# A mixture-of-experts layer in 48 half tiles instead of 64, with its weights loaded by SyncE

## What is computed

```python
x = hidden_states.reshape(-1, h)                      # 2048 x 512
p = jax.nn.sigmoid(x @ gate_w.T)                      # 16 experts
p = p / jnp.sum(p, axis=-1, keepdims=True)
w, idx = jax.lax.top_k(p, 2)
w = w / jnp.sum(w, axis=-1, keepdims=True)
combine = jnp.sum(one_hot(idx, 16) * w[..., None], axis=1)
gu = jnp.einsum('th,ehf->etf', x, gate_up_proj)       # 512 -> 2 x 256
gate, up = jnp.split(gu, 2, axis=-1)
inter = jax.nn.silu(gate) * up
y = jnp.einsum('eti,eih->eth', inter, down_proj)      # 256 -> 512
out = jnp.einsum('eth,te->th', y, combine)
```

## Time and profile before

| | us |
|---|---|
| median of three runs | 2494.53 |
| the profiled execution, its time | 2495.26 |
| the profiled execution, span of its records | 2495.2 |
| of it, up to the start of the expert loop | 2118 |
| the expert loop, 64 steps | 328 |
| behind the last product | 49 |

### The profile page before, as it was taken

The page is one execution under the profiler, slowest core; times in us unless marked ns, Lnnn a source line. Parts: engine busy times, 40 slices in busy tenths (PEclk is TensorE's granted clock), DMA queues, the critical chain, the costliest instruction groups (busy, mean ns, idle before and its releaser), DMA issues. The chain is left out here.

```text
span 2495.2 us, 40462 instructions
## 1 busy us (share of the span) xinstructions
PE 2258.1 (90%) x12755; PEld 1950.1 (78%) x12755; DVE 1629.1 (65%) x3963; ACT 1238.8 (50%) x3351; POOL 719.4 (29%) x1299
## 2 busy tenths in 40 slices
PE   4999999999995789977999999999999964999992
PEld 4999899999884567766888888888888852878781
DVE  5777777777778952234666666666666676666664
ACT  3545545545543112215666666666666631666661
POOL 1000100100000642223333333433333302666672
PEclk8999999999997999998999999999999986999996
DMA  6111121211101310001111111111211012566405
GB/s 232 60 66 53 59 71 63 71 59 48 65 35 31 94 32 0 0 24 61 43 51 48 70 50 42 67 42 50 72 46 42 35 55 73 205 224 228 156 3 202
DMA packets 77784, 182.74 MB, mean 73 GB/s; under 512 B 13936, under 2 KB 44680, under 8 KB 65952
## 3 DMA queue, kind: packets, MB, share of 16 engines
q1 hardware_dynamic: 57376, 127.46, 14.6%
q0 software_dynamic: 20352, 54.58, 6.2%
HBM read 186.17 MB, written 29.36 MB: 86 GB/s over the span
## 5 line engine op out<-in xcount | busy, mean ns | idle before, releaser
L502 PE MATMUL bank<-l_wkv_hi,l_ctxT 128*128 128x256 f32 (+1 forms) x1024 | 280.3, 346 | 9.4 <-PEq L135 9.0
L791 DVE TENSOR_TENSOR l_v_lo<-bank,l_v_hi 128x128 fp32r<-128x128 f32 (+1 forms) x256 | 91.7, 358 | 223.5 <-ACT l_v_hi L688 222.2
L791 DVE TENSOR_TENSOR l_pT_lo<-bank,l_pT_hi 128x512 fp32r<-128x512 f32 x256 | 175.3, 685 | 81.8 <-ACT l_pT_hi L713 81.8
L502 PE MATMUL bank<-l_wo_hi,l_oT_hi 128*128 128x512 f32 x528 | 216.7, 410 | 3.3 <-DVE l_oT_lo L791 2.8
L707 ACT ACTIVATE l_probs<-l_scored,l_nbias 128x256 f32<-128x256 f32 x256 | 128.2, 502 | 166.8 <-DVE l_nbias L844 163.4
L502 PE MATMUL bank<-xnT_hi,l_wq_hi 128*128 128x512 f32 x512 | 210.1, 410 | 0.0
L502 PEld LDWEIGHTS bank<-l_wkv_hi,l_ctxT 128*128 128x128 f32 x1024 | 184.1, 194 | 30.9 <-issue 9.4
L502 PE MATMUL bank<-l_wo_lo,l_oT_hi 128*128 128x512 f32 x528 | 208.0, 394 | 0.0
L502 PE MATMUL bank<-l_wo_hi,l_oT_lo 128*128 128x512 f32 x528 | 207.0, 392 | 0.0
L502 PE MATMUL bank<-xnT_hi,l_wq_lo 128*128 128x512 f32 x512 | 203.2, 397 | 0.0
L502 PE MATMUL bank<-xnT_lo,l_wq_hi 128*128 128x512 f32 x512 | 202.3, 395 | 0.0
(11 more groups left out here) (237 smaller groups left out, 6431.2 us busy)
## 6 DMA issues: line engine op xcount, KB each, us to landing
l_ctxT<-ctx_split SPq DMA_DIRECT2D x64, 1024.0 KB, 4.8
l_raw_a<-in_L_xattn_Wq SPq DMA_DIRECT2D x16, 512.0 KB, 5.6
l_raw_a<-in_L_xattn_Wo SPq DMA_DIRECT2D x16, 512.0 KB, 5.4
moe_raw_gu<-moe_y_rows SPq DMA_DIRECT2D x8, 1024.0 KB, 6.4
x_sb<-in_x SPq DMA_DIRECT2D x4, 1024.0 KB, 11.3
ctx_split<-ct SPq DMA_DIRECT2D x4, 1024.0 KB, 11.3
xn_rows<-xn SPq DMA_DIRECT2D x16, 256.0 KB, 2.4
out_x<-x_sb SPq DMA_DIRECT2D x8, 512.0 KB, 3.3
```

The source lines that it names most:

```text
L502: mm = nc.tensor.matmul(out, a[x], b[y], start=(i == 0), stop=(i == n - 1))
L791: nc.vector.tensor_tensor(pair[1], src, pair[0].bitcast(F32), ALU.subtract).then_inc(done, 1)
```

## The change

Experts get tiles of two sizes. Sixteen pair tiles hold 256 rows, sixteen single tiles 128. An expert's full 256 rows go into pair tiles; a rest over 128 rows goes into a pair tile while there are any left, and otherwise into two single tiles; a smaller rest into one single tile. The order of work is pair, single, pair, single, so three halves belong together and there are 48 steps (`HALVES`), written out without a hardware loop; waits are on constants. For a tile that no row needs, the expert's number is now 15, so its weights are loaded too.

SyncE loads the weights: it reads the expert's number from SBUF into a register (`value_load`) and issues plain DMAs with that offset. GpSimd issues the row gathers and the scatters only, straight from `token_of` and `dest_of`. There are three buffers for rows and three for outputs instead of four. TensorE waits for the weights of gate and up in two parts, and for each gather of rows by itself. At the end six buffers take the loads of output rows (the raw weights' two and the four split ones), and ScalarE issues the stores.

Of the diff, the constants, the loads, the programs of GpSimd and TensorE, the arithmetic that sorts rows into tiles, and the end:

```diff
-            rows_out = [k.sem(f"ln_rows_out{i}") for i in range(2)]
+            rows_out = k.rows_out = [k.sem(f"ln_rows_out{i}") for i in range(2)]
...
+    PAIRS = T // P
+    HALVES = 3 * PAIRS
+    STEPS = 3
...
+            def load_gate_up(b, j):
+                due(sp, wg_split[b], 2 * j)
+                e = sp.value_load(expert_of[0:1, PAIRS * b + j:PAIRS * b + j + 1], min_val=0, max_val=E - 1)
+                sp.dma_start(raw_gu[b][:, :], gu_v[bass.ds(e, 1), :, :].rearrange("o p c -> (o p) c")).then_inc(gu_in[b], 16)
...
+            sp.wait_ge(experts_set, 1)
+            load_gate_up(0, 0)
+            load_gate_up(1, 0)
+            load_down(0, 0)
+            for j in range(PAIRS):
+                if j + 1 < PAIRS:
+                    load_gate_up(0, j + 1)
+                load_down(1, j)
+                if j + 1 < PAIRS:
+                    load_gate_up(1, j + 1)
+                    load_down(0, j + 1)
+
+            for b in y_out:
+                sp.wait_ge(b, 16 * PAIRS)
             yv = y_rows.rearrange("(t p k) d -> p t (k d)", p=P, k=2)
...
             for n in range(NT // 2):
...
+                due(sp, summed, 2 * (n - 5))
+                sp.dma_start(both_rows[n % 6].rearrange("p (t c) -> p t c", t=2), yv[:, 2 * n:2 * (n + 1), :]).then_inc(both_in[n % 6], 16)
...
+            def gather_rows(n):
+                due(pool, x_turned, n - 2)
                 apart(k, pool)
...
+                at = bass.IndirectOffsetOnAxis(ap=token_of[:, column_of(n)], axis=0)
+                gp.indirect_dma_start(rows[n % STEPS][:, :], None, xn_rows, at, bounds_check=T - 1,
+                                      oob_is_err=False).then_inc(rows_in[n % STEPS], 16)
+
+            def scatter(n):
+                pool.wait_ge(y_copied, n + 1)
                 apart(k, pool)
...
+                at = bass.IndirectOffsetOnAxis(ap=dest_of[:, column_of(n)], axis=0)
+                gp.indirect_dma_start(y_rows, at, y_sb[n % STEPS][:, :], None, bounds_check=2 * T - 1, oob_is_err=False).then_inc(y_out[n % STEPS], 16)
+
+            pool.wait_ge(listed, 2)
+            for n in range(HALVES + STEPS):
+                if n < HALVES:
+                    gather_rows(n)
+                if n >= STEPS:
+                    scatter(n - STEPS)
...
+            def turn_x(n):
+                pe.wait_ge(rows_in[n % STEPS], 16 * (n // STEPS + 1))
+                due(pe, x_split, n - 1)
+                by_feature = rows[n % STEPS][:, :].rearrange("p (q k) -> p k q", k=KD)
...
+            pe.wait_ge(listed, 2)
+            turn_x(0)
+            for n in range(HALVES):
+                if n + 1 < HALVES:
+                    turn_x(n + 1)
+                gate_up_products(n)
+                if n >= 1:
+                    turn_f(n - 1)
+                if n >= 2:
+                    down(n - 2)
...
+            def copy_y(n):
+                act.wait_ge(y_made, n + 1)
+                due(act, y_out[n % STEPS], 16 * (n // STEPS))
+                nc.scalar.copy(y_sb[n % STEPS][:, :], b_y[n % 2][:, :]).then_inc(y_copied, 1)
...
+            for n in range(NT // 2):
+                act.wait_ge(summed, 2 * (n + 1))
+                act.dma_start(ov[:, 2 * n:2 * (n + 1), :], k.x_sb[:, 2 * n:2 * (n + 1), :]).then_inc(stored, 16)
...
+            rounded(full[:, :], rows_of, 0.5 / P, (1 - 2 * P) / 4 / P)
+            chain(v.scalar_tensor_tensor(rest[:, :], full[:, :], -2.0 * P, rows_of, ALU.mult, ALU.add))
+            chain(v.tensor_scalar(big[:, :], rest[:, :], float(P), None, ALU.is_gt))
+            chain(v.tensor_scalar(rest[:, :], rest[:, :], 0.0, None, ALU.is_gt))
+            chain(v.tensor_reduce(room[:, :], full[:, :], AX.X, ALU.add))
+            chain(v.tensor_scalar(room[:, :], room[:, :], -1.0, float(PAIRS), ALU.mult, ALU.add))
+            prefix(paired, big)
+            chain(v.scalar_tensor_tensor(paired[:, :], paired[:, :], room[:, :], big[:, :], ALU.is_le, ALU.mult))
+            chain(v.tensor_tensor(pairs[:, :], full[:, :], paired[:, :], ALU.add))
+            prefix(pair_end, pairs)
```

More of the change, by code:

```diff
@@ L1257, in moe_stage @@
                              "picked", "ranked", "experts_set", "sorted", "tabled", "listed"))
[L1258 to L1261, removed]
+        gu_in, dn_in, wg_hi, wg_split, wd_hi, wd_split = (
+            [sem(f"{n}{i}") for i in range(2)] for n in ("gu_in", "dn_in", "wg_hi", "wg_split", "wd_hi", "wd_split"))
@@ L1281, in iterations, with due @@
[L1281 to L1291, removed]
+        def due(eng, s, n):
+            if n > 0:
+                eng.wait_ge(s, n)
+        both_rows = [raw_gu[0][:, :], raw_gu[1][:, :]] + [w[i][:, :].bitcast(F32) for w in w_gu for i in range(2)]
         def one_hots(c):
@@ L1364, in scatter @@
[L1364 to L1386, removed]
@@ L1441, in gate_up_products @@
                 for c in range(KD):
+                    if n % STEPS != 1 and c % 2 == 0:
+                        pe.wait_ge(wg_split[b], 2 * j + 1 + c // 2)
                     for x, w in ((0, 0), (0, 1), (1, 0)):
-                        mm = nc.tensor.matmul(b_gu[s % 2][:, :], xT[s % 2][x][:, c, :], w_gu[b][w][:, 2 * I * c:2 * I * (c + 1)],
-                                              start=(j == 0), stop=(j == 3 * KD - 1))
-                        j += 1
+                        mm = nc.tensor.matmul(b_gu[n % 2][:, :], xT[n % 2][x][:, c, :], w_gu[b][w][:, 2 * I * c:2 * I * (c + 1)],
+                                              start=(i == 0), stop=(i == 3 * KD - 1))
+                        i += 1
@@ L1494, in _, with copy_x @@
                 nc.scalar.activation(probT[:, GT * g:GT * (g + 1)], banks[g][0:E, :], ACT.Sigmoid).then_inc(sigmoids_made, 1)
[L1496 to L1501 removed]
+            def copy_x(n):
+                act.wait_ge(x_turned, n + 1)
+                due(act, gu_made, n - 1)
+                nc.scalar.copy(xT[n % 2][0], b_x[n % 2][:, :].rearrange("p (k t) -> p k t", k=KD)).then_inc(x_hi, 1)
@@ L1548, in _ @@
-            iterations(act, body)
-            end = (None, ITER)
-            copy_f(*step(end, -1))
-            copy_y(*step(end, -2))
-            copy_y(*step(end, -1))
+                weights_gate_up(0, 0, c)
+            copy_x(0)
+            for n in range(HALVES):
+                s, j = n % STEPS, n // STEPS
+                if n + 1 < HALVES:
+                    copy_x(n + 1)
+                if s < 2:
+                    weights_gate_up(1, j, s)
+                elif j + 1 < PAIRS:
+                    weights_gate_up(0, j + 1, 0)
+                    weights_gate_up(0, j + 1, 1)
+                else:
+                    weights_down(1, j)
+                if s == 0 and j >= 1:
+                    weights_down(1, j - 1)
+                if s == 1:
+                    weights_down(0, j)
+                gate(n)
+                if n >= 1:
+                    copy_f(n - 1)
+                if n >= 2:
+                    copy_y(n - 2)
@@ L1618, in _, with prefix @@
-            tiles = column[:, 0:LISTED].rearrange("p (j o) -> p j o", o=1).broadcast_to([P, LISTED, E])
-            chain(v.tensor_tensor(passed[:, :, :], tiles, over_t(last_tile[:, :], LISTED), ALU.is_ge))
-            chain(v.tensor_reduce(found[:, :], passed[:, :, :], AX.X, ALU.add))
-            chain(v.tensor_scalar(found[:, :], found[:, :], float(P), part, ALU.mult, ALU.add))
-            chain(v.tensor_copy(expert_of[:, :], found[:, :]))
-            for b in range(2):
-                v.tensor_copy(gather_at[b][:, HALVES:HALVES + 1], expert_of[:, b:b + 1]).then_inc(experts_set, 1)
+            def prefix(ends, counted):
+                chain(v.tensor_tensor(spread, after[:, :, :], over_t(counted[:, :], E), ALU.mult))
+                chain(v.tensor_reduce(ends[:, :], spread, AX.X, ALU.add))
@@ new lines, in _ @@
+            prefix(single_end, singles)
+            tiles = column[:, 0:PAIRS].rearrange("p (j o) -> p j o", o=1).broadcast_to([P, PAIRS, E - 1])
+            for b, ends in enumerate((pair_end, single_end)):
+                chain(v.tensor_tensor(passed[:, :, :], tiles, over_t(ends[:, 0:E - 1], PAIRS, E - 1), ALU.is_ge))
+                chain(v.tensor_reduce(found[:, PAIRS * b:PAIRS * (b + 1)], passed[:, :, :], AX.X, ALU.add))
+            v.tensor_copy(expert_of[:, :], found[:, :]).then_inc(experts_set, 1)
@@ new lines, in _ @@
+            for c in range(2):
+                lo_gate_up(0, 0, c)
+            lo_x(0)
+            for n in range(HALVES):
+                s, j = n % STEPS, n // STEPS
+                if n + 1 < HALVES:
+                    lo_x(n + 1)
+                if s < 2:
+                    lo_gate_up(1, j, s)
+                elif j + 1 < PAIRS:
+                    lo_gate_up(0, j + 1, 0)
+                    lo_gate_up(0, j + 1, 1)
+                else:
+                    lo_down(1, j)
+                if s == 0 and j >= 1:
+                    lo_down(1, j - 1)
+                if s == 1:
+                    lo_down(0, j)
```

(3 more changed lines are left out.)

323 lines of the change are left out of this document (108 added, 215 removed).

## The result

The changed kernel takes 2768.56 us, the median of four runs (2767.32 to 2771.07), against 2494.9 us for the kernel before on the same chip: a ratio of 1.111, 95% interval 1.109 to 1.112. It is slower by 11%; 2780 was forecast. The profiled execution has a span of 2769.1 us, 273.9 more than before.

The account below looks back on a forecast made before the run. The prediction took TensorE to bound the expert loop before the change. From 2495.2 us, +290.1 for the loop, +3.2 before it and -9 after it gave 2779.5, forecast as 2780 us, range 2685 to 2872.

Parts of the forecast that it names:

- the stage: The whole expert loop: forecast 617.4 us against 327.3 before, +290.1 us.
- the clock's term: Expert loop: waits lower TensorE's clock to 1.2 GHz at each step's start, 2.2 us a step (1.4 to 3.0).
- Zero lead: Expert loop: gather n waits behind scatter n-4, so TensorE waits a whole round 44 times, half 4 to 47.
- The round: Expert loop, each step's wait: output copied, scatter issued, gather issued, rows landed; 6.44 us (5.1 to 7.7).
- Step and stage: Expert loop: a step of 4.89 + 6.44 + 2.2 = 13.5 us (11.4 to 15.6), 44 times, 594 us.
- Before the loop: Ahead of the expert loop: longer slot arithmetic, less smaller one-hot operations, index copy and one gather's wait; +3.2 us.
- After the loop: Result rows read back with six buffers, loads queued at once: -9 us (-5 to -13).
- At nothing: Changes priced at zero: GpSimd's lost weight gathers and branches, SyncE's weight loads, weight splitting, fetching the unrolled program.
- a clock that stays high: Rival, expert loop: waits too short to lower the clock, step 11.3 us, 2683 us in all; chance 10%.
- The faster case: Rival, expert loop: rows arrive in time, the beat stays at 4.89 us, 2401 us in all; chance 4%.
- weights or fetches: Rival, expert loop: late weights or instruction fetches also stop TensorE, up to 30 us more, 2810 us; chance 8%.

Follow-up runs that it names:

- filler: Changed kernel plus 22 unread 512-column products ahead of each turning from half 4 on: 2716.85 us; the same with 60 of 64 weight loads left out: 2671.26 us.
- the fastest kernel: Changed kernel with GpSimd's scatter standing five halves behind the gather (scatter n-5 instead of n-3): 2404.81 us, ratio 0.963.
- the three placings: Scatter n-5 kernel with GpSimd gathering weights by index: behind the scatter 2462.0 us, ahead of it 2425.2, ahead and one step earlier 2439.54.

## Why the prediction was right

The forecast of 2780 us is 11.4 us above the median, 0.4%, and its own sum of 2779.5 is 10.4 above the profiled span: the stage was put 8.7 too high, the part before it 0.9 too low, the part behind it 2.6 too high. The range was 187 us wide, so a hit this close has luck in it: the clock's term was a choice of the middle, and a step 0.3 us too long was made up in part by a first round that was longer than the others. Step by step:

- **Zero lead.** That gather n stands behind scatter n-4, which waits for the last work of the step before, is what the circle in the chain shows, and moving the scatter by one and by two half tiles confirmed it: step 13.2, 6.4 and 4.96 us. This was read from the two programs, not from a duration, and it decided the sign.
- **The round, 6.44 us.** The full one shown above is 0.02 + 0.59 + 0.87 + 1.02 + 0.30 + 3.39 + 0.04 = 6.2 (2411.52 to 2417.77). The mean from half 5 on is 5.93, since gathers of mostly empty slots land sooner (2.14 us at 2441.66, when the queue moved 0.13 MB instead of the 0.48 of the gather above). The first round, of half 4, took 10.1. The one choice in it, 3.44 for a landing that no row showed in a loaded loop, held at 3.3, in a loop so slow that the gather is nearly alone; at twice the pace it would have been 4.1 (median) to 4.7. The Trainium skill's figures (DMA: Bandwidth & Descriptors, "Anatomy of one DMA — SWDGE (gpsimd) path") had led to an estimate of 2.6 us, and the trace doesn't agree for this gather: it has 3.3.
- **The clock, 2.2 us a step.** From the turning to the end of the down products a step takes 7.26 us against 4.89: 2.4. With filler the step became 2.1 us shorter. The middle between the two slow times of the earlier trace rows, 4.9 us, was a choice without a row behind it, and it came out well: in the step shown above the products follow each other at the slow pace from 2417.77 to about 2422.9. But the clock is not low from the start of the wait; it falls at its end, as the busy times of the step show. The Trainium skill's rule of a clock that falls before every group (TensorE: Matmul & The Clock Gate, "HAM oscillation — how this bites in real kernels") stood for this too, and the trace agrees: 0.50 at the start of the burst, 0.76 on the mean.
- **Step and stage.** 13.5 us forecast, 5.93 + 7.26 = 13.19 measured; 617.4 us against 608.7. The shorter steps take 13 us off the forecast, and the start with its long first round gives 5 back.
- **Before the loop, +3.2.** The loop starts 4.1 us later, but 1.3 of that is there before VectorE's first operation of the routing (2078.85 against 2077.56), and the change doesn't touch what stands there. What is left is 2.8 against the 3.2. The slot arithmetic, put at 11.1 us, runs from 2090.26 to 2101.14, 10.9.
- **After the loop, -9.** It was -11.6, and -12 by itself on the kernel before. The mis-sized term is the rate of the transfers: 359 GB/s came from a stretch with one load and one store in flight; with all loads queued the mean of 2736 to 2762 us was 404. From the issue of the first load to the end it took 34.6 us where 36.5 were forecast. The chain still ends in a load for which VectorE waits (the 17.54 us above), so the transfers stay the bound: 12.6 MB at 404 GB/s are 31 us, an estimate, and some us of start and end come on top. The stretch in front of the first load shrank by 1.8 us, not by 1.
- **At nothing.** The weights cost next to nothing, shown by leaving them out (-5 us at most). No wait for fetched code stands in the waits, and the fastest kernel, just as long, runs at 4.96 us a step.

The rivals: a clock that stays high (2683) is near the kernel whose clock does stay high, 2671 without the weight loads; with them it was 2717. Here the clock fell. The faster case, 2401 with rows in time, is the kernel with the scatter five behind, 2405. That weights or fetches add up to 30 us didn't happen.

## What to carry to other kernels

For each transfer that an in-order engine issues, count the lead in work of the engine that waits for it: find what stands ahead of it in the program, what that waits for, and how many steps lie between that event and the use. The circle (copy, wake, issues, landing, and the work in it) divided by the number of steps that it spans is the floor of the step: here 13.2 us for one, 6.3 for two, and below TensorE's own 4.89 for three. Moving a scatter by two places was worth 364 us, without any more memory, while a fourth row buffer and the absence of the weight loads bought next to none of it; and once the loop is fast again, price the transfers anew, since they then meet.

## What the runs showed of the hardware

- A gather of 128 rows by index lands in 3.3 us (median) where the loop is slow and 4.1 at a step of 6.4 us. Where the weights are gathered by the same queue it took 5.4, 4.2 and 4.7 us in the three placings, so the queue alone doesn't set it. A weight load of 1 MB goes from 4.8 us in the slow loop (104 GB/s in all) to 6.7 in the fastest (277 GB/s).
- With a wait of 6 us before each burst of 7 us the granted clock went up and down once a step, between 0.50 and 1.00, with a mean of 0.76: still 1.00 in most of the idle wait, 0.50 in most of the burst. With TensorE kept busy in the wait it was 1.00. Work that nobody reads bought 93 us without the weight loads and 52 with them.
- The loads of the result rows, six buffers queued at once, and the stores beside them ran at 404 GB/s on the mean, above the 359 of the earlier trace rows.
